# Attention norm in an eight-core attention and FFN kernel: the reciprocal row reaches 64 partitions by a DMA from SBUF to SBUF instead of fp32 matmuls and copies

## The reference

```python
q = jnp.concatenate([q_content, q_rope], axis=-1)      # 16 heads, 64 + 32
k = jnp.concatenate([k_content, k_rope], axis=-1)
scores = jnp.einsum('bhqd,bhkd->bhqk', q, k) * scale   # T = 2048
scores = jnp.where(causal[None, None], scores, -jnp.inf)
attn = jax.nn.softmax(scores, axis=-1)
out = jnp.einsum('bhqk,bhkd->bhqd', attn, v)
return out.transpose(0, 2, 1, 3).reshape(Bx, Tx, 1024) @ W_o
```

## Time and profile before

| | us |
|---|---|
| runs of the kernel | 3892.41 and 4030.39, median 3961.4 |
| profiled execution | 3893.95 |
| its span, core 0 (the slowest of 8: 3844.6 to 3892.1) | 3892.1 |
| attention stage, first QK to last norm | 550 to 1228 |
| PE busy over the span | 2798.3 (72%) |
| ACT busy | 1422.5 (37%) |
| DVE busy | 1244.4 (32%) |

### The profile page before, as it was taken

One profiled execution on the slowest core, in us unless ns is written; L12 is line 12 of the kernel. 1 busy time (PEld: TensorE's weight loads), 2 busy tenths in 40 slices (PEclk: granted clock), 3 DMA queues, 4 the chain that ended last, 5 costly groups with the idle time before them and its releaser, 6 DMA issues.

```text
span 3892.1 us, 41211 instructions; the slowest of 8 cores (3844.6 to 3892.1 us)
## 1 busy us (share of the span) xinstructions
PE 2798.3 (72%) x12144; PEld 1188.5 (31%) x12144; DVE 1244.4 (32%) x2606; ACT 1422.5 (37%) x2337; POOL 216.7 (6%) x208
## 2 busy tenths in 40 slices
PE   2476766776778777887478887886887839769843
PEld 1131122222223334443133333333444214324312
DVE  6456740000001474443701101175443531101112
ACT  1101336666664256771123033045775113103110
POOL 0000000000000220000000000030000000000030
PEclk9986687777768875558689999995555969889875
DMA  2401220000001300000083183110000045255134
GB/s 67 81 1 44 63 63 25 17 17 25 17 17 49 92 1 1 1 1 11 0 115 48 19 109 57 30 26 1 1 2 12 0 55 84 34 69 77 28 113 146
DMA packets 117340, 157.54 MB, mean 40 GB/s; under 512 B 31578, under 2 KB 84444, under 8 KB 116106
## 3 DMA queue, kind: packets, MB, share of 16 engines
q0 software_dynamic: 86624, 82.83, 15.0%
q1 hardware_dynamic: 30508, 72.08, 6.0%
HBM read 208.35 MB, written 29.36 MB: 61 GB/s over the span
## 4 chain that ended last, share of the span: by engine, by line
PE 52%; DVE 14%; DMA 12%; ACT 11%; issue 8%; POOL 1%; SPq 1%; DVEq 0%; ACTq 0%; POOLq 0%
PE P L1703 8%; PE P L1637 7%; PE P L1645 7%; PE P L505 4%; PE P L921 4%; PE P L873 4%; ACT pn L1346 3%; DVE misc L1342 3%; PE P L963 2%; DMA w1a<-w 2%; DMA w2b<-w 2%; PE P L1369 2%; PE P L1400 2%; DMA x_ld<-x 2%; PE P L1504 2%
## 5 line engine op out<-in xcount | busy, mean ns | idle before, releaser
L1637 PE MATMUL P<-hln,w1a 128*128 128x512 bf16 (+1 forms) x1408 | 340.6, 386 | 159.5 <-DMA w1a<-w 159.5
L887 ACT ACTIVATE ptb<-P,misc 128x1024 bf16<-128x1024 f32 (+7 forms) x384 | 321.3, 864 | 131.6 <-PE P L873 76.9
L1645 PE MATMUL P<-hln,w1g 128*128 128x512 bf16 (+1 forms) x1408 | 333.8, 380 | 12.1 <-DMA w1g<-w 11.2
L1656 ACT ACTIVATE asc<-P,lt_g 128x512 bf16<-128x512 f32 (+1 forms) x176 | 120.9, 687 | 555.4 <-PE P L1637 423.2
L1670 DVE TENSOR_TENSOR mid<-asc,glu 128x512 bf16<-128x512 bf16 (+1 forms) x176 | 74.9, 425 | 660.9 <-ACT glu L1663 660.9
L921 PE MATMUL P<-ptb,v 128*65 128x512 bf16 (+3 forms) x640 | 226.9, 426 | 34.6 <-DVE attnT L975 34.2
L975 DVE TENSOR_TENSOR attnT<-P,bcn_sb 64x1024 bf16<-64x1024 f32 x32 | 39.0, 1217 | 640.0 <-ACT bcn_sb L969 640.0
L873 PE MATMUL P<-qh,kh 96*128 96x512 bf16 (+3 forms) x640 | 212.1, 401 | 41.9 <-ACT ptb L887 28.5
L1637 PEld LDWEIGHTS P<-hln,w1a 128*128 128x128 bf16 (+1 forms) x1408 | 139.0, 99 | 334.1 <-issue 174.0
L1703 PE MATMUL P<-mid,w2a 128*128 128x512 bf16 x704 | 171.3, 394 | 84.8 <-DMA w2b<-w 84.8
L1354 ACT ACTIVATE pz<-pn,misc 128x640 bf16<-128x640 bf16 (+4 forms) x256 | 194.8, 761 | 98.4 <-DVE misc L1351 92.7
(11 more groups left out here) (204 smaller groups left out, 3676.4 us busy)
## 6 DMA issues: line engine op xcount, KB each, us to landing
w1a<-w POOLq DMA_DIRECT2D x16, 1024.0 KB, 11.2
w1g<-w POOLq DMA_DIRECT2D x16, 1024.0 KB, 15.4
w2a<-w POOLq DMA_DIRECT2D x4, 2816.0 KB, 21.7
w2b<-w POOLq DMA_DIRECT2D x4, 2560.0 KB, 18.7
xstage<-x SPq DMA_DIRECT2D x16, 512.0 KB, 3.9
s_scratch<-s_stage SPq DMA_DIRECT2D x32, 256.0 KB, 2.5
s_ld<-s_scratch SPq DMA_DIRECT2D x8, 1024.0 KB, 5.9
x_ld<-x SPq DMA_DIRECT2D x16, 512.0 KB, 4.2
```

Source lines behind the costliest of these rows:

```text
L887: ex = p.s(lambda e, pt=pt, off=off, lspan=lspan, pb=pb: e.activation(out=pt_sb[pb][:, 0:lspan], in_=pt[:, off:off + lspan], func=AF.Exp, ...
L1637: sla=sla, hlo=hlo, w1a=w1a: e.matmul(sla[0][0:wdt, sla[1]:sla[1] + 512], w1a[jj][:, k * gw + mi * 128: k * gw + mi * 128 + wdt], hln[:, k ...
L1645: slg=slg, hlo=hlo, w1g=w1g: e.matmul(slg[0][0:wdt, slg[1]:slg[1] + 512], w1g[jj][:, k * gw + mi * 128: k * gw + mi * 128 + wdt], hln[:, k ...
```

## The change

The two matmuls and two copies of a norm are replaced by one DMA on SP, with a source that reads the same 1024 values 64 times (step 0) and 64 partitions as destination. It waits for both reciprocals and for the multiplication that last read bcn_sb. The multiplication waits for the DMA; `rec_war` now holds the DMA, so that L943 waits for it before it writes the slot again.

```diff
         oj = h % 2
         ot_off = oj * 1024
-        bp = P3 if j == 0 else P2
-        bb = bank_of(bp, 512)
-        be = []
-        bms = []
-        for half2 in range(2):
-            bm = p.t(lambda e, half2=half2, base=base, bp=bp: e.matmul(
-                bp[0:64, 512:1024], ones_row[0:1, 0:64],
-                rec_row[0:1, base + half2 * 512: base + (half2 + 1) * 512],
-                start=True, stop=True), waits=[rcs[half2]] + pw_waits([bb]))
-            pw_done([bb], bm)
-            bms.append(bm)
-            bev = p.s(lambda e, half2=half2, bp=bp: e.copy(
-                out=bcn_sb[0:64, half2 * 512:(half2 + 1) * 512],
-                in_=bp[0:64, 512:1024]), waits=[bm, bcn_free[0]])
-            pr_done([bb], bev)
-            be.append(bev)
-        rec_war[j] = bms[-1]
+        src_b = vap(rec_row, base, [(0, 64), (1, 1024)])
+        tbc = p.ydma(lambda e, src_b=src_b: e.dma_start(
+            out=bcn_sb[0:64, 0:1024], in_=src_b),
+            waits=rcs + [bcn_free[0]], chain="bcn")
+        be = [tbc]
+        rec_war[j] = tbc
```

## The result

The changed kernel takes 3943.07 us (median of 13 runs) against 3898.66 us before (10 runs). The ratio is 1.0115, 95% interval 1.0097 to 1.0133: 1.15% slower, clear of noise and inside the 2% that counts as the same. By the profiled time of before that is +45 us, where +68 was forecast. The ratio leaves disturbed runs of both kernels out.

What follows compares the result with a forecast made beforehand. Waits, not a full engine, were taken to bound the attention stage. Fifteen periods +52.8 us, first head +7.1 and last head +7.9 gave +68 us on 3893.95, so 3962 us; range 3912 to 4060 us.

Steps and rivals of the forecast that it cites:

- B's gap of 6.8 us: Behind a head's second-pass norm, before the change: ACT could go on at about 675.0 but starts at 681.84, on 15 heads.
- B: The norm after a head's second query pass; the next head uses P1's other half, so its first PV needs nothing of it.
- D: Time from SP's issue of the broadcast DMA to its landing: 1.5 us fixed plus 10.0 us data, 11.5 us.
- The estimate by the Trainium skill's port figure: Broadcast DMA at 27.6 GB/s for one port: 9.5 us for 262 KB, and a sum some 16 us lower.
- The 32-partition row: Earlier trace's transfer from 32 source partitions: engines 0.98 busy, only 215 GB/s; by 8 ports, 27 GB/s each.
- The series of B and A: One bcn_sb makes A's DMA wait for B's multiplication, 3.2 us late; both norms take 25.84 us from B's reciprocals.
- A: The norm after a head's first query pass; the next pass's first PV must wait until L975 has read P1.
- From resumption to the next B: From PE's resumption after A to B's reciprocals: 19.86 us, unchanged, with PE's granted clock at 0.50 for the first 5 us.
- The hop to PE: From the end of A's multiplication L975 to PE's resumption: 0.14 us.
- Full speed: First rival: the broadcast DMA reads its row as fast as from 128 partitions; -132 us, 3762 us; chance 0.12.
- Engines that disturb each other: Rival: in every broadcast DMA, 16 engines read one partition at half rate; 320 us more, 4282 us; chance 0.09.
- Not spread: Rival: all 64 packets of the broadcast DMA on one engine; +97 us, 3991 us; counted into the forecast case's 0.79.

## Why the prediction was right

- **No engine is full, waits set the stage.** Right. 123 us less of PE and 35 us less of ACT came with a longer stage.
- **B's gap of 6.8 us goes.** Right: the exponentials follow at once (682.06), and B alone by DMA gained 2.2%. The transfer behind it is hidden.
- **D = 11.5 us.** Measured 11.0. Fixed part 1.3 us (11.0 - 9.67), the lower of the two ends, where 1.5 was taken; data 9.67 instead of 10.0, 262,144 bytes at 27 GB/s where the earlier trace rows had shown at least 24. At 32 a microsecond this is 16 of the 23 us by which the sum was too high. The mechanism was right, one source that all engines share, but that the number came so close is partly luck: the 24 GB/s of the earlier trace rows are the rate of one engine, while the 27 are that of a port, and nothing in the rows said that the two would be near each other. The estimate by the Trainium skill's port figure, D about 11.0 and 16 us lower, was the better one. The 32-partition row had told the same: its 27 GB/s per port are the rate found here.
- **The series of B and A.** Right in place and size. 25.84 us were given from B's reciprocals to the end of A's multiplication, 24.87 measured (682.03 to 706.90). The run with two buffers took the series away.
- **From resumption to the next B, 19.86 us unchanged.** Too long: the mean of the changed kernel is 19.24, 9 us less over the periods. About half of that is the choice of head. 19.86 was read at the one head of the earlier trace rows; over all 15 periods of the kernel before, the distance runs from 19.07 to 20.00, with a mean of 19.54. It goes with the granted clock behind the resumption: the heads that have 0.50 in the first 5.26 us, as the one in the earlier trace rows, take 19.85 to 20.00 us, the others, with 0.58 to 0.66, 19.07 to 19.61. One of those, of the kernel before:

```profile
570.29:575.55 5.26, 5.26 (x15) 2.16 (x16) 0.00 (x0) 2.50 (x3) 0.00 (x0) 0.59 0.00 0
```

  In the changed kernel all heads of the slowest core have 0.59 to 0.61 (0.62 to 0.69 on core 0), as this one:

```profile
662.82:668.08 5.26, 5.26 (x15) 2.06 (x16) 0.00 (x0) 2.60 (x3) 0.00 (x0) 0.61 0.01 3
```

  PE's 1.2 GHz stretch ends about 1 us sooner there than at the head of the earlier trace rows. In the run with two buffers it varies again by head, from 0.50 to 0.72, and the mean distance is 19.39. So the forecast's assumption, 0.50 behind every resumption, did not even hold before the change. Why no head of the changed kernel has 0.50 is open.
- **The hop to PE.** 0.28 us instead of 0.14 (706.90 to 707.18), +2 us. It is the only one of the three differences that goes the other way, so the sum did not come out by errors that cancel.
- **The sum.** 15 x 2.06 = 31 us over the periods (52.8 forecast); the first head from reciprocals to PE 12.70 us against 5.92, +6.8 (7.1); the last from reciprocals to the end of the multiplication 12.46 against 4.99, +7.5 (7.9). In all +45, and the ratio gives +45.
- **L921 waits some 15 us each, 240 in all.** 17.9 each, 286.0 in all. The figure did not follow from the sum: PE is idle from its last QK, without L963 in between, not from where it used to wait.
- **The rivals.** Full speed: excluded, and its price confirmed by the run with 64 source partitions. Engines that disturb each other: excluded, 16 engines share 27 GB/s without loss (with four engines it is 25). Not spread: excluded by the share of 0.86. One bound in the first rival is slightly off: A waits for B's multiplication from D = 9.76 - 1.42 = 8.3 us on, not 8.2. Nothing else hangs on it.

## What to carry to other kernels

A transfer costs what waits for it: the same 11 us were free behind one pass and, in series, left PE idle for 17.9 us behind the other, and the buffer that the next pass writes decides which. Before replacing engine work by a DMA that repeats one row, divide all its bytes, not the row's, by about 27 GB/s, and add the 1.3 us measured here for issue and landing; halving the width of the data, or rows that lie several partitions apart, changes the answer. Where a consumer stalls right behind a norm, first look whether the next pass could go to another accumulator: that made a losing change a gain of 3.6%.

## What the runs showed of the hardware

- A DMA with 64 packets of 4 KB from one SBUF partition runs at 27 GB/s on 16 engines, 11.0 us in all; from 64 partitions to the same destination it lands in 2.9 us.
- From four neighbouring partitions 25 GB/s, from four with a step of 32 49 GB/s, with a step of 4 73 GB/s, each on four engines.
- A source whose outer dimension is 4 used four engines (share 0.23 to 0.24), though the destination had 64 partitions.
- A DMA of a repeated row takes SP 0.47 us to issue, and 0.54 with the four-partition source, against 0.31 for a plain load of kh.
